# Second layer: key and query projections of one pair with high and low parts of x in one 512-column matmul

## The chip, the cores and the metric

The kernel runs on one core of one Trainium2 chip. The metric is the device time of one execution in microseconds (us). Three executions of the kernel before took 2110.76, 2111.51 and 2111.34 us, median 2111.34.

## The reference

Two conditioned transformer blocks in fp32, one after the other, on x of 64 sequences, 128 rows, 512 features, with a condition vector of 1024 per sequence. The first block has linear attention with 8 heads, the second has softmax attention with 16 heads of 32 features. The second block is the one that matters here:

```python
xn = layer_norm(x, norm_w, norm_b)
q = (xn @ q_w + q_b).reshape(Bx, Tx, H, -1)
k = (xn @ k_w + k_b).reshape(Bx, Tx, H, -1)
att = softmax(einsum('bnhl,bmhl->bnmh', q, k) + (1 - mask) * -1e6, axis=2)
y = einsum('bnmh,bmhl->bnhl', att, v).reshape(Bx, Tx, Dx)
h = layer_norm(y, sb_norm_w, sb_norm_b) * (1 + scale) + shift
return x + silu(h) @ out_w + out_b
```

`v` is a third projection of `xn`; `scale` and `shift` come from the condition vector.

## The kernel before, in words

Sequences go in pairs: 32 pairs through the first layer, then 32 pairs through the second. A tile has 128 partitions; D = 512 features are C = 4 chunks of 128, `b` is the sequence in the pair. The x of the next pair is loaded, normalised and transposed while the present pair is in attention.

Every projection is made from two parts of each operand. `xT_hi` is x in the reduced type fp32r, `xT_lo` is the rest, and the same for the weights `w_hi` and `w_lo`. The product is hi·hi + lo·hi + hi·lo, so three matmuls for each chunk, accumulated in one PSUM bank. `project_features` (L539) does this for keys and queries, with the weights stationary and 256 columns of x (2 sequences of 128) moving: one block `f` of 128 output features fills half a bank of 512 columns. `project_rows` (L531) does it for values and the output, with x stationary and 512 columns of weights moving.

Each engine has a program of its own, in one fixed order, and semaphores order them against one another. There is no planner. In the second layer each pair `i` has two steps, one for each of its sequences:

- `step0` (TensorE, L1752): scores of sequence 0, output of the previous pair's sequence 0, values, transposes of z, of prob and of the next x (`x_transposed`), output of the previous pair's sequence 1, mixing (`mixed`).
- `step1` (TensorE, L1780): scores of sequence 1; then keys of the next pair, blocks 0 and 1 woven with the four transposes of y (`turned`), blocks 2 and 3; transposes of z (`z_transposed`, L1631); query blocks 0 and 1; the 16 transposes of prob (`prob_turned`); query blocks 2 and 3; `mixed`.

The banks: 0 to 3 hold scores, then transposed prob. 4 is for y, 7 for z, 5 and 6 for keys, then queries, values, x (5, 7) and output (6).

VectorE in `step1` (L1432): maxima of score banks 0, 1, 2 (L1342); `end_outputs` (L1346: reciprocal of the sums, z from y, its statistics); maximum of bank 3; `keys_out` for blocks 0 and 1 (L1327: bank plus bias into `qk`); `end_norm` (L1370: normalise z, after GpSimd's 1/sqrt, L1234); `keys_out` 2 and 3; statistics of the x after next (`row_stats`); `end_silu`; `norm`; `low_part`.

ScalarE in `step1` (L1597): copy of y; 16 exponentials with their sums (`exps`, four heads for each bank); `gate` for z (L1530, four operations that read the transposed z); tanh; `queries_out` 0, 1 (L1498); copy of prob bank 0; `h_high`; the other three copies of prob; `queries_out` 2, 3.

`step1` of the first pair (`first`) also has the second layer's gains in it: TensorE transposes them (`emb.turned`) into bank 7, VectorE takes them out in eight small operations (`leave_bank`, L508), and makes them up (`gains`, L518). The last pair has no next one, so its `step1` projects nothing. So 31 of 32 pairs have the projections in `step1`.

Of the kernel before, what the change touches and what calls it, by code (L numbers as in the profile page):

```python
# [44 lines left out]
def build(nc, T, out):  # L45
# [15 lines left out]
    with root:  # L61
# [30 lines left out]
        m.xT_hi = sb("xT_hi", [P, C, PAIR, P], F32R)  # L92
        m.xT_lo = sb("xT_lo", [P, C, PAIR, P], F32R)
# [43 lines left out]
        def vcol(name, c):  # L137
# [11 lines left out]
            "x_biased", "qk_ps", "k", "q", "masks_in", "v_ps", "v", "s_ps", "top", "prob", "pT_ps", "pT",  # L149
# [990 lines left out]
def layer1(nc, m, s0, s, ps, T, emb, x1_d, out, x_in, mask_d, vec_rows, vcol, B, NP, D, C, HC, H, DH):  # L1140
# [33 lines left out]
    Y_BANK, Z_BANK, O_BANK = 4, 7, 6  # L1174
    QK_BANKS, V_BANKS, X_BANKS = (5, 6), (5, 6), (5, 7)
# [3 lines left out]
    def qk_banks(pair, n):  # L1179
        return FIRST_QK_BANKS[n] if isinstance(pair, int) and pair == 0 else QK_BANKS  # L1180
# [124 lines left out]
    def vector(dve):  # L1305
# [21 lines left out]
        def keys_out(pair, chunks):  # L1327
            banks = qk_banks(pair, K)
            for c in chunks:
                if c % 2 == 0:  # L1330
                    dve.wait_ge(s["qk_ps"], seq(C, pair, c // 2 + 1))
                at = (c % 2) * PAIR * P
                done = nc.vector.tensor_scalar(qk[:, K, c].rearrange("p b t -> p (b t)"),
                                               ps[banks[c // 2]][:, at:at + PAIR * P], qk_bias[:, K, c:c + 1],
                                               None, ALU.add)
                if c % 2:
                    done.then_inc(s["k"], 1)
# [94 lines left out]
        def step1(i, first, more, last):  # L1432
            maxima(i, 1, (0, 1, 2))
            end_outputs(i, 0)
            maxima(i, 1, (3,))
            if first:
                emb.leave_bank(dve, ps[Z_BANK])
            if not last:
                keys_out(i + 1, (0, 1))
            end_norm(i, 0)  # L1440
            if first:
                emb.gains(dve)
            if not last:
                keys_out(i + 1, (2, 3))
# [24 lines left out]
        keys_out(0, range(C))  # L1469
# [22 lines left out]
    def scalar(act):  # L1492
# [5 lines left out]
        def queries_out(pair, chunks):  # L1498
            banks = qk_banks(pair, Q)
            for c in chunks:  # L1500
                if c % 2 == 0:
                    act.wait_ge(s["qk_ps"], seq(C, pair, 2 + c // 2 + 1))
                at = (c % 2) * PAIR * P
                done = nc.scalar.activation(qk[:, Q, c].rearrange("p b t -> p (b t)"),
                                            ps[banks[c // 2]][:, at:at + PAIR * P], ACT.Identity,
                                            bias=qk_bias[:, Q, c:c + 1])
                if c % 2:
                    done.then_inc(s["q"], 1)

        def exps(i, b, first):  # L1510
            for a in range(HC):
# [18 lines left out]
        def gate(prev, b, bank=Z_BANK):  # L1530
# [47 lines left out]
        queries_out(0, (0, 1))  # L1578
        yield
        queries_out(0, (2, 3))  # L1580
# [16 lines left out]
        def step1(i, first, last):  # L1597
            copy_yT(i, 0)
            exps(i, 1, first)
            gate(i, 0)  # L1600
            tanh(i, 0)
            if not last:
                queries_out(i + 1, (0, 1))
            prob_out(i, 1, (0,))
            h_high(i, 0)
            prob_out(i, 1, (1, 2, 3))
            if not last:
                queries_out(i + 1, (2, 3))
# [15 lines left out]
    def tensor(pe):  # L1624
# [6 lines left out]
        def z_transposed(prev, b, bank=Z_BANK):  # L1631
# [13 lines left out]
        def projected(pair, n, chunks):  # L1645
            banks = qk_banks(pair, n)
            for f in chunks:
                dst = ps[banks[f // 2]][:, (f % 2) * PAIR * P:(f % 2 + 1) * PAIR * P]
                done = None
                for done in project_features(nc, w_hi, w_lo, n, f, xT_hi, xT_lo, dst, C, True):  # L1650
                    yield
                if f % 2:
                    done.then_inc(s["qk_ps"], 1)
# [7 lines left out]
        def scores(i, b):  # L1661

            if b == 0:
                pe.wait_ge(s["masks_in"], seq(16 * HC, i, 16 * HC))
                pe.wait_ge(s["q"], seq(2, i, 2))
                pe.wait_ge(s["k"], seq(2, i, 2))
# [21 lines left out]
        def mixed(i, b, first):  # L1688

            pe.wait_ge(s["v"], seq(PAIR, i, b + 1))  # L1690
            if b == 1:
                pe.wait_ge(s["y"], seq(PAIR, i, 1))
            elif not first:
# [47 lines left out]
        run(projected(0, K, range(C)))  # L1741
        pe.wait_ge(s["lo_qk"], 2)
        run(projected(0, Q, (0, 1)))
        yield
        run(projected(0, Q, (2, 3)))
# [34 lines left out]
        def step1(i, first, last):  # L1780
# [5 lines left out]
            else:  # L1786
                pe.wait_ge(s["xT_lo"], seq(PAIR, i + 1, PAIR))
                if first:
                    emb.turned(pe, ps[Z_BANK])
                woven(projected(i + 1, K, (0, 1)), turned(i, 0))  # L1790
                if not first:
                    pe.wait_ge(s["out"], seq(PAIR, i - 1, PAIR))
                run(projected(i + 1, K, (2, 3)))
                if first:
                    pe.wait_ge(emb.s["scale"], 1)
                z_transposed(i, 0)
                pe.wait_ge(s["k"], seq(2, i + 1, 1))
                run(projected(i + 1, Q, (0, 1)))
                prob_turned(i, 1, range(HC))
                pe.wait_ge(s["k"], seq(2, i + 1, 2))  # L1800
                run(projected(i + 1, Q, (2, 3)))
# [41 lines left out]
```

## Time and profile before

| | before |
|---|---|
| median of 3 executions | 2111.34 us |
| profiled execution, its own time | 2112.14 us |
| its span | 2110.3 us |
| mean granted TensorE clock | 0.996 |
| TensorE busy | 2071.9 us (98%) |
| VectorE busy | 1395.6 us (66%) |
| ScalarE busy | 1155.9 us (55%) |
| GpSimd busy | 581.8 us (28%) |

The span runs from the first to the last instruction; the execution's own time has 1.8 us around it. The second layer begins at about 1012 us. The busy time of TensorE includes the modelled ends of its matmuls, which overlap, so the distance between two starts is the price of a matmul, not its own duration. Granted clock is a share of 2.4 GHz.

### The profile page before, as it was taken

The page shows a single profiled execution, that of the slowest core. Times are in us where ns is not written, and L with a number is a line of the kernel's source. Part 1 is how long each engine was busy: PE and PEld are TensorE (multiplying, and loading weights), DVE is VectorE, ACT ScalarE, POOL GpSimd, SP SyncE. Part 2 cuts the span into 40 slices and gives each one's busy share as a digit, 9 for nine tenths or more (in the row PEclk, how much of TensorE's full clock was granted, in tenths as well). Part 3 has the DMA queues.
Part 4 walks back from the last instruction along what each step waited for, and adds up shares of the span by engine and source line. Part 5 has one row for each costly group of instructions (what it writes and reads, how often), then busy time and mean ns, then how long its engine had stood idle before and what let it go on. Part 6 is the DMA issues. An engine that isn't in the chain of part 4 may idle for free. (4 is left out here: it accounts for less than half of the span.)

```text
span 2110.3 us, 48285 instructions
## 1 busy us (share of the span) xinstructions
PE 2071.9 (98%) x17499; PEld 1824.0 (86%) x17499; DVE 1395.6 (66%) x2985; ACT 1155.9 (55%) x3816; POOL 581.8 (28%) x861
## 2 busy tenths in 40 slices
PE   7999999999999999999999999999999999999996
PEld 4888888888888888888798989899898989899895
DVE  6777777777777777776565656666565556656553
ACT  3333433343333433344677777777777777777774
POOL 4233323333233322334222222222222222222220
PEclk9999999999999999999999999999999999999998
DMA  6310001101110011102210101101010100101000
GB/s 214 110 40 30 35 35 40 40 25 35 40 40 31 33 35 40 40 25 76 66 36 25 35 25 35 40 22 38 25 35 25 35 29 31 40 25 35 25 26 21
DMA packets 52164, 86.43 MB, mean 41 GB/s; under 512 B 5667, under 2 KB 14565, under 8 KB 52134
## 3 DMA queue, kind: packets, MB, share of 16 engines
q1 hardware_dynamic: 52118, 86.03, 11.9%
q8 instruction: 19, 0.31, 0.1%
q14 instruction: 11, 0.09, 0.0%
q10 hardware_dynamic: 16, 0.00, 0.0%
HBM read 52.32 MB, written 33.69 MB: 41 GB/s over the span
## 5 line engine op out<-in xcount | busy, mean ns | idle before, releaser
L543 PE MATMUL bank<-xT_hi,w_hi 128*128 128x256 f32 x1536 | 449.4, 293 | 0.0
L544 PE MATMUL bank<-xT_lo,w_hi 128*128 128x256 f32 x1536 | 439.8, 286 | 0.0
L545 PE MATMUL bank<-xT_hi,w_lo 128*128 128x256 f32 x1536 | 437.0, 284 | 0.0
L1515 ACT ACTIVATE heads<-bank,top 128x128 f32<-128x128 f32 x1024 | 358.2, 402 | 100.5 <-DVE top L1342 100.5
L534 PE MATMUL bank<-w_hi,xT_hi 128*128 128x512 f32 x768 | 306.3, 399 | 4.4 <-DVE bias_all L395 4.4
L536 PE MATMUL bank<-w_lo,xT_hi 128*128 128x512 f32 x768 | 301.9, 393 | 0.0
L535 PE MATMUL bank<-w_hi,xT_lo 128*128 128x512 f32 x768 | 301.1, 392 | 0.0
L543 PEld LDWEIGHTS bank<-xT_hi,w_hi 128*128 128x128 f32 x1536 | 293.1, 191 | 6.2 <-issue 1.6
L544 PEld LDWEIGHTS bank<-xT_lo,w_hi 128*128 128x128 f32 x1536 | 293.4, 191 | 0.8 <-issue 0.8
L545 PEld LDWEIGHTS bank<-xT_hi,w_lo 128*128 128x128 f32 x1536 | 293.6, 191 | 0.0
L1342 DVE TENSOR_REDUCE top<-bank 128x4 f32<-128x512 f32 x256 | 162.7, 677 | 179.7 <-PE bank L1675 179.7
L927 ACT ACTIVATE heads<-bank,k_neg 128x128 f32<-128x128 f32 x256 | 70.1, 370 | 355.6 <-DVE k_neg L792 355.6
L1515 ACT ACTIVATION_READ_ACCUMULATOR heads<-bank,top 128x1 f32 x1024 | 248.5, 243 | 0.0
L534 PE MATMUL bank<-w_hi,h_hi 128*128 128x512 f32 x512 | 217.6, 425 | 9.1 <-DVE h_lo L1381 5.1
L535 PE MATMUL bank<-w_hi,h_lo 128*128 128x512 f32 x512 | 212.0, 414 | 0.0
L536 PE MATMUL bank<-w_lo,h_hi 128*128 128x512 f32 x512 | 206.2, 403 | 0.0
L534 PEld LDWEIGHTS bank<-w_hi,xT_hi 128*128 128x128 f32 x768 | 144.8, 189 | 33.0 <-DVE bias_all L395 4.9
L536 PEld LDWEIGHTS bank<-w_lo,xT_hi 128*128 128x128 f32 x768 | 144.6, 188 | 31.2
L535 PEld LDWEIGHTS bank<-w_hi,xT_lo 128*128 128x128 f32 x768 | 144.9, 189 | 28.6 <-issue 0.2
L695 POOL TENSOR_TENSOR h_lo<-ends,h_hi 128x512 fp32r<-128x512 f32 x64 | 86.8, 1376 | 219.9 <-ACT h_hi L953 219.9
L1522 ACT ACTIVATE heads<-bank 128x512 f32<-128x512 f32 x256 | 141.3, 599 | 2.8 <-PE bank L1685 2.3
L1232 POOL TENSOR_TENSOR ve_y<-mv_y,eps 128x1 f32<-128x1 f32 x64 | 12.2, 190 | 424.0 <-DVE mv_y L1360 424.0
(201 smaller groups left out, 4057.5 us busy)
## 6 DMA issues: line engine op xcount, KB each, us to landing
xr<-in_x SPq DMA_DIRECT2D x32, 512.0 KB, 3.4
x_between_layers<-ends SPq DMA_DIRECT2D x64, 256.0 KB, 2.0
xr<-x_between_layers SPq DMA_DIRECT2D x32, 512.0 KB, 4.1
out<-ends SPq DMA_DIRECT2D x64, 256.0 KB, 2.1
store<-in_L_cond_W_emb SPq DMA_DIRECT2D x4, 1024.0 KB, 12.1
store<-in_L_cond_emb_w SPq DMA_DIRECT2D x3, 1024.0 KB, 8.3
mask_rows<-mask_parts SPq DMA_DIRECT2D x128, 2.0 KB
heads<-in_L_cond_Wk SPq DMA_DIRECT2D x1, 1024.0 KB, 6.9
```

The source lines that it names most:

```text
L534: yield nc.tensor.matmul(bank[:, :], a_hi[:, c, b, :], w_hi[:, m, c, :], start=(c == 0), stop=False)
L535: yield nc.tensor.matmul(bank[:, :], a_lo[:, c, b, :], w_hi[:, m, c, :], start=False, stop=False)
L536: yield nc.tensor.matmul(bank[:, :], a_hi[:, c, b, :], w_lo[:, m, c, :], start=False, stop=(c == C - 1))
L543: yield nc.tensor.matmul(dst, w_hi[:, m, c, fs], a_hi[:, c], start=(first and c == 0), stop=False)
L544: yield nc.tensor.matmul(dst, w_hi[:, m, c, fs], a_lo[:, c], start=False, stop=False)
L545: yield nc.tensor.matmul(dst, w_lo[:, m, c, fs], a_hi[:, c], start=False, stop=(last and c == C - 1))
L695: nc.gpsimd.tensor_tensor(h_lo[:, :, b, :], hs[:, b], f32(h_hi[:, :, b, :]), ALU.subtract).then_inc(s["h_lo"], 1)
L927: last = nc.scalar.activation(k_exp[:, c, b, :], ps[j][:, at:at + P], ACT.Exp, bias=k_neg[:, c, b:b + 1])
L1232: nc.gpsimd.tensor_tensor(ve_y[:, b:b + 1], mv_y[:, b, 1:2], eps[:, 0:1], ALU.add).then_inc(s["y_var_eps"], 1)
L1342: nc.vector.tensor_reduce(top[:, b, C * a:C * a + C], ps[a][:, :].rearrange("p (c t) -> p c t", c=C), AX_X, ALU.max, negate=True).then_inc ...
L1515: last = nc.scalar.activation(prob[:, a, c, :], ps[a][:, c * P:(c + 1) * P], ACT.Exp, bias=top[:, b, h:h + 1], accum_out=total[:, b, h:h + 1])
L1522: nc.scalar.activation(prob_T[:, a], ps[a][:, :].rearrange("p (c t) -> p c t", c=C), ACT.Copy).then_inc(s["pT"], 1)
```

## The change

- `xT_hi` and `xT_lo` become views of one tile `xT`, laid out chunk, part (high, low), sequence, row.
- For all pairs but the first, key blocks 0 to 3 and query blocks 0 and 1 go through `project_wide`: for each chunk one matmul of `w_hi` with the 512 columns of high and low x, into a whole bank, and one of `w_lo` with the 256 columns of high x, into the bank's lower half. The block is then the sum of the bank's halves.
- ScalarE writes lower half plus bias into `qk` (`lower_out`), then VectorE adds the upper half to it (`block_out`). Query blocks 2 and 3 stay in the old form (`narrow`), in the halves of bank 5, and ScalarE copies both (`queries_out`).
- Banks: keys 5, 6, 7, 5; queries 6, 7, 5, 5. z of sequence 0 is transposed into bank 4, of sequence 1 into bank 7.
- TensorE's `step1`: key 0 woven with y's transposes, keys 1, 2, 3, z, queries 0, 1, prob, queries 2, 3. New waits: for VectorE's first key block before key 3, second before query 0, third before query 1; for the gates before `mixed` of sequence 1; in the first pair the gains leave bank 7 before key 2 rather than before z.
- VectorE's and ScalarE's `step1` get a new order, shown below. Semaphores `k`, `q` and `qk_ps` count blocks, not pairs of blocks; `lower` is new.

```diff
+def project_wide(nc, w_hi, w_lo, m, f, both, dst, C):
+    fs = slice(f * P, (f + 1) * P)
+    n = PAIR * P
+    for c in range(C):
+        yield nc.tensor.matmul(dst[:, :], w_hi[:, m, c, fs], both[:, c].rearrange("p h b t -> p (h b t)"),
+                               start=(c == 0), stop=False)
+        yield nc.tensor.matmul(dst[:, 0:n], w_lo[:, m, c, fs], both[:, c, 0].rearrange("p b t -> p (b t)"),
+                               start=False, stop=(c == C - 1))
...
+    Z_BANKS = (4, 7)
+    QK_BANKS, V_BANKS, X_BANKS = ((6, 7, 5, 5), (5, 6, 7, 5)), (5, 6), (5, 7)
...
+        def block_out(pair, n, f):                                   # VectorE
+            dst = qk[:, n, f].rearrange("p b t -> p (b t)")
+            dve.wait_ge(s["lower"], seq(C + 2, pair - 1, (K, Q).index(n) * C + f + 1))
+            nc.vector.tensor_tensor(dst, ps[QK_BANKS[n][f]][:, PAIR * P:2 * PAIR * P], dst,
+                                    ALU.add).then_inc(s["k" if n == K else "q"], 1)
...
         def step1(i, first, more, last):                            # VectorE
             maxima(i, 1, (0, 1, 2))
+            if not last:
+                block_out(i + 1, K, 0)
             end_outputs(i, 0)
             maxima(i, 1, (3,))
             if first:
+                emb.leave_bank(dve, ps[EMB_BANK])
+            if not last:
+                block_out(i + 1, K, 1)
             end_norm(i, 0)
+            if not last:
+                block_out(i + 1, K, 2)
+                block_out(i + 1, K, 3)
             if first:
                 emb.gains(dve)
             if more:
                 row_stats(i + 2, slot_of(i + 2))
+            if not last:
+                block_out(i + 1, Q, 0)
             end_silu(i, 0)
+            if not last:
+                block_out(i + 1, Q, 1)
             if more:
                 norm(i + 2, slot_of(i + 2))
             low_part(i, 0)
...
+        def lower_out(pair, n, f):                                   # ScalarE
+            act.wait_ge(s["qk_ps"], seq(EACH, pair, (K, Q).index(n) * C + f + 1))
+            nc.scalar.activation(qk[:, n, f].rearrange("p b t -> p (b t)"), ps[QK_BANKS[n][f]][:, 0:PAIR * P],
+                                 ACT.Identity, bias=qk_bias[:, n, f:f + 1]).then_inc(s["lower"], 1)
...
         def step1(i, first, last):                                  # ScalarE
             copy_yT(i, 0)
+            exps(i, 1, first, (0, 1))
+            if not last:
+                lower_out(i + 1, K, 0)
+            exps(i, 1, first, (2,))
+            if not last:
+                lower_out(i + 1, K, 1)
+                lower_out(i + 1, K, 2)
+            exps(i, 1, first, (3,))
+            if not last:
+                lower_out(i + 1, K, 3)
             gate(i, 0)
             tanh(i, 0)
+                lower_out(i + 1, Q, 0)
             prob_out(i, 1, (0,))
             h_high(i, 0)
+            prob_out(i, 1, (1,))
+                lower_out(i + 1, Q, 1)
+            prob_out(i, 1, (2, 3))
+                queries_out(i + 1, 2)
+                queries_out(i + 1, 3)
...
+                woven(projected(K, 0), turned(i, 0))                 # TensorE, step1
                 if not first:
                     pe.wait_ge(s["out"], seq(PAIR, i - 1, PAIR))
+                else:
+                    emb.turned(pe, ps[EMB_BANK])
+                run(projected(K, 1))
                 if first:
                     pe.wait_ge(emb.s["scale"], 1)
+                run(projected(K, 2))
+                pe.wait_ge(s["k"], seq(C, i + 1, 1))
+                run(projected(K, 3))
                 z_transposed(i, 0)
+                pe.wait_ge(s["k"], seq(C, i + 1, 2))
+                run(projected(Q, 0))
+                pe.wait_ge(s["k"], seq(C, i + 1, 3))
+                run(projected(Q, 1))
                 prob_turned(i, 1, range(HC))
+                pe.wait_ge(s["k"], seq(C, i + 1, C))
+                narrow(Q, 2)
+                narrow(Q, 3)
```

## Rows read from the trace of the kernel before

**Rows 1.** Busy time by stretch: us, then per engine busy (instructions), granted clock, DMA.
```profile
1400.00:2100.00 700.00, 689.76 (x6832) 618.16 (x6824) 411.93 (x831) 505.49 (x1887) 154.00 (x257) 0.99 0.09 30
...
1004.00:1012.00 8.00, 7.99 (x34) 6.49 (x35) 1.44 (x2) 0.00 (x0) 2.34 (x3) 1.00 0.78 262
2083.70:2095.30 11.60, 9.44 (x63) 7.76 (x64) 2.45 (x5) 6.45 (x19) 0.00 (x0) 0.65 0.01 1
```

**Rows 2.** Waits of TensorE, whole span: us in total, times, longest.
```profile
PE bank L1635 <- DVE z L1372: 5.9, 3, 4.8
```

**Rows 3.** Timeline of TensorE, one pair: start, duration, line, tiles, count [idle before].
```profile
1501.63 0.50 PE L1669 MATMUL bank<-mask_rows,one_rows 2*128 2x512 f32 x4
...
1504.10 0.28 PE L545 MATMUL bank<-xT_hi,w_lo 128*128 128x256 f32 x1
...
1509.14 0.28 PE L545 MATMUL bank<-xT_hi,w_lo 128*128 128x256 f32 x1
1509.26 0.60 PE L1635 MATMUL bank<-ident,z 128*128 128x128 f32 x4
...
1517.27 1.08 PE L1698 MATMUL bank<-heads,v 128*32 128x128 f32 x32
1518.28 0.50 PE L1669 MATMUL bank<-mask_rows,one_rows 2*128 2x512 f32 x4
```

**Rows 4.** Timeline of TensorE, value rows of the next step.
```profile
1522.95 0.40 PE L534 MATMUL bank<-w_hi,xT_hi 128*128 128x512 f32 x1
...
1525.49 0.39 PE L536 MATMUL bank<-w_lo,xT_hi 128*128 128x512 f32 x1
```

**Rows 5.** Timeline of VectorE in the same pair.
```profile
1500.90 0.69 DVE L1389 TENSOR_TENSOR ends<-bank,xr 128x512 f32<-128x512 f32 x1 [1.41 <-issue]
1503.06 1.89 DVE L1342 TENSOR_REDUCE top<-bank 128x4 f32<-128x512 f32 x3 [1.47 <-PE bank L1675]
1504.86 0.24 DVE L1348 RECIPROCAL p_sum<-total 128x16 f32<-128x16 f32 x1
...
1506.75 0.66 DVE L1342 TENSOR_REDUCE top<-bank 128x4 f32<-128x512 f32 x1
1507.33 0.87 DVE L1333 TENSOR_SCALAR pairs<-bank,qk_bias 128x256 f32<-128x256 f32 x2
1508.11 0.54 DVE L1372 TENSOR_SCALAR z<-z,mv_y,rstd_y 128x512 f32<-128x512 f32 x1
```

**Rows 6.** Timeline of ScalarE in the same pair.
```profile
1503.78 0.37 ACT L1515 ACTIVATE heads<-bank,top 128x128 f32<-128x128 f32 x1 [1.42 <-DVE top L1342]
...
1506.54 0.41 ACT L1515 ACTIVATE heads<-bank,top 128x128 f32<-128x128 f32 x1
...
1509.96 1.50 ACT L1536 ACTIVATE gates<-bank,gains 128x128 f32<-128x128 f32 x4 [0.49 <-PE bank L1635]
1511.49 0.63 ACT L1542 ACTIVATE gates<-gates 128x512 f32<-128x512 f32 x1
...
1514.50 1.58 ACT L1522 ACTIVATE heads<-bank 128x512 f32<-128x512 f32 x3
1517.38 0.84 ACT L1504 ACTIVATE pairs<-bank,qk_bias 128x256 f32<-128x256 f32 x2 [1.30 <-PE bank L545]
```

**Rows 7.** Timeline of GpSimd in the same pair.
```profile
1507.18 0.55 POOL L1234 TENSOR_TENSOR rstd_y<-ve_y,neg_half 128x1 f32<-128x1 f32 x1
```

**Rows 8.** Timeline of VectorE in the first pair.
```profile
1032.93 0.27 DVE L514 TENSOR_SCALAR store<-bank,vec 128x64 f32<-128x64 f32 x1
...
1034.36 0.25 DVE L522 TENSOR_SCALAR half_gain<-store,vec 128x64 f32<-128x64 f32 x1
```

**Rows 9.** Timeline of TensorE at three places where it idled.
```profile
1004.01 0.49 PE L534 MATMUL bank<-w_hi,h_hi 128*128 128x512 f32 x1 [2.39 <-POOL h_lo L695]
...
1044.57 0.50 PE L1669 MATMUL bank<-mask_rows,one_rows 2*128 2x512 f32 x4 [0.86 <-DVE w_lo L1395]
...
2083.74 1.12 PE L1635 MATMUL bank<-ident,z 128*128 128x128 f32 x4 [4.75 <-DVE z L1372]
```

More of the change, by code:

```diff
@@ L1325, in x_low, with first_keys_out @@
                                     f32(xT_hi[:, :, b, :]), ALU.subtract).then_inc(s["xT_lo"], 1)
[L1327 to L1337, printed above, removed]
+        def first_keys_out():
+            for c in range(C):
+                dve.wait_ge(s["qk_ps"], c // 2 * 2 + 2)
+                nc.vector.tensor_scalar(qk[:, K, c].rearrange("p b t -> p (b t)"), first_block(K, c),
+                                        qk_bias[:, K, c:c + 1], None, ALU.add).then_inc(s["k"], 1)
+        def block_out(pair, n, f):
[3 more added lines that the diff above has]
+                                    ALU.add).then_inc(s["k" if n == K else "q"], 1)
         def maxima(i, b, some):
@@ L1468, in vector @@
         yield
-        keys_out(0, range(C))
+        first_keys_out()
         low(V)
@@ L1496, in x_high, with first_queries_out, queries_out, exps @@
                                  ACT.Copy).then_inc(s["xT_hi"], 1)
-        def queries_out(pair, chunks):
-            banks = qk_banks(pair, Q)
+        def first_queries_out(chunks):
             for c in chunks:
[L1501 to L1511, printed above, removed]
+                act.wait_ge(s["qk_ps"], C + c // 2 * 2 + 2)
+                nc.scalar.activation(qk[:, Q, c].rearrange("p b t -> p (b t)"), first_block(Q, c), ACT.Identity,
+                                     bias=qk_bias[:, Q, c:c + 1]).then_inc(s["q"], 1)
+        def lower_out(pair, n, f):
+            act.wait_ge(s["qk_ps"], seq(EACH, pair, (K, Q).index(n) * C + f + 1))
+            nc.scalar.activation(qk[:, n, f].rearrange("p b t -> p (b t)"), ps[QK_BANKS[n][f]][:, 0:PAIR * P],
+                                 ACT.Identity, bias=qk_bias[:, n, f:f + 1]).then_inc(s["lower"], 1)
+        def queries_out(pair, f):
+            act.wait_ge(s["qk_ps"], seq(EACH, pair, EACH))
+            at = (f % 2) * PAIR * P
+            nc.scalar.activation(qk[:, Q, f].rearrange("p b t -> p (b t)"),
+                                 ps[QK_BANKS[Q][f]][:, at:at + PAIR * P], ACT.Identity,
+                                 bias=qk_bias[:, Q, f:f + 1]).then_inc(s["q"], 1)
+        def exps(i, b, first, some=range(HC)):
+            for a in some:
                 act.wait_ge(s["top"], seq(PAIR * C, i, b * C + a + 1))
@@ L1528, in copy_yT, with gate @@
                                  ACT.Copy).then_inc(s["yT"], 1)
-        def gate(prev, b, bank=Z_BANK):
+        def gate(prev, b, bank=None):
+            bank = Z_BANKS[b] if bank is None else bank
             if b == 0:
@@ L1629, in x_transposed, with z_transposed @@
             last.then_inc(s["xT_ps"], 1)
-        def z_transposed(prev, b, bank=Z_BANK):
+        def z_transposed(prev, b, bank=None):
+            bank = Z_BANKS[b] if bank is None else bank
             pe.wait_ge(s["z"], seq(PAIR, prev, b + 1))
@@ L1643, in out_rows, with first_projected, projected, narrow @@
             done.then_inc(s["o_ps"], 1)
-        def projected(pair, n, chunks):
-            banks = qk_banks(pair, n)
+        def first_projected(n, chunks):
             for f in chunks:
[L1648 to L1653, printed above, removed]
+                run(project_features(nc, w_hi, w_lo, n, f, xT_hi, xT_lo, first_block(n, f), C, True))\
+                    .then_inc(s["qk_ps"], 1)
+        def projected(n, f):
+            done = None
+            for done in project_wide(nc, w_hi, w_lo, n, f, m.xT, ps[QK_BANKS[n][f]], C):
+                yield
+            done.then_inc(s["qk_ps"], 1)
+        def narrow(n, f):
+            dst = ps[QK_BANKS[n][f]][:, (f % 2) * PAIR * P:(f % 2 + 1) * PAIR * P]
+            run(project_features(nc, w_hi, w_lo, n, f, xT_hi, xT_lo, dst, C, True)).then_inc(s["qk_ps"], 1)
         def value_rows(i, b):
@@ L1740, in tensor @@
         pe.wait_ge(s["lo_qk"], 1)
-        run(projected(0, K, range(C)))
+        first_projected(K, range(C))
         pe.wait_ge(s["lo_qk"], 2)
-        run(projected(0, Q, (0, 1)))
+        first_projected(Q, (0, 1))
         yield
-        run(projected(0, Q, (2, 3)))
+        first_projected(Q, (2, 3))
         pe.wait_ge(s["lo_vo"], 1)
```

42 lines of the change are left out of this document (15 added, 27 removed).

## The prediction

> **What bounds the kernel now.** I read the busy shares by stretch first. In 700 us of the second layer TensorE is busy 98.5% at full clock, ScalarE 72%, VectorE 59% [rows 1]. The list of waits says the same from the other side: over the whole span the transposes of z wait for VectorE only 3 times out of 64 [rows 2], and the one place of a pair where TensorE's stream waits at all is before the scores: ScalarE's last query copies end at 1517.38 + 0.84 = 1518.22 and the scores start at 1518.28, 0.2 us later than the matmuls before them would let them [rows 3, 6]. So TensorE's issue order is the clock of the layer, and an edit is worth what it does to TensorE's stream. Then I read the timeline of one pair, the steady step 1 that begins with the scores at 1501.63 and ends with the next scores at 1518.28 (16.65 us) [rows 3]. All 31 steps 1 that project a next pair have this shape; the last pair has none.
>
> The point to see there is how closely the other engines feed that stream. The z transposes start at 1509.26, and VectorE's z was written from 1508.11 for 0.54 us, to 1508.65 [rows 3, 5]. Today that is 0.5 us early. There is no other slack on this chain, and the edit adds to exactly this chain.
>
> **The edit on TensorE.** Of 32 blocks-by-chunks of keys and queries per pair (8 blocks, 4 chunks) 24 now issue one 512-column and one 256-column matmul in place of three 256-column ones. The columns streamed are the same, 768. From 1504.10 to 1509.14 are 42 intervals of 256 columns, so 120.0 ns each; from 1522.95 to 1525.49 are 11 intervals of 512 columns, so 230.9 ns each [rows 3, 4]. One merge saves 240.0 - 230.9 = 9.1 ns, so 16 merges in the keys save 0.15 us and 8 in the queries 0.07 us. That is 0.22 us a pair, 6.8 us over 31 pairs, and it is all that the edit can give. From below I take nothing saved (a 512 followed by a 256 with another weight has no row). The four transposes of y woven into the first key block cost what they cost today. The new order of banks adds TensorE no wait of its own in the keys: bank 6 is free at 1501.59 (VectorE's addition to the output starts at 1500.90 and takes 0.69) and is wanted only after the first key block [rows 5].
>
> In sentences of their own: the Trainium skill ("TensorE: Matmul & The Clock Gate", Back-to-back issue gap) gives N/2.4 ns + 2.5 ns between warm matmuls, thus 109.2 and 215.8 ns, and a merge would save only 2.6 ns. The rows do not agree with its size, they show 9.1 ns. By that rule the queries' part would be 0.02 us in place of 0.07 and the sum below 1.6 us longer.
>
> **The edit on VectorE and ScalarE, up to z.** This is the term that decides. VectorE's program after the maxima of score banks 0 to 2 was: reciprocal, z product, its statistics, maximum of bank 3, two key blocks, normalise z. Now the addition for key block 0 stands ahead of the reciprocal. It waits for ScalarE's lower half of that block, and ScalarE issues it only after the exponentials of banks 0 and 1. Both queues run in order, so everything of z stands behind it. Step by step, in the times of the pair shown:
> - The three maxima start at 1503.06 and take 1.89, to 1504.95 [rows 5].
> - The first exponential starts at 1503.78, the ninth at 1506.54 [rows 6]. ScalarE's lower half takes the ninth's place at 1506.54. Two copies of that size take 0.84 [rows 6], one alone about 0.47, so it ends at 1507.01. TensorE had finished that block long before, near 1505.
> - VectorE, idle since 1504.95, starts the addition at 1507.06. No row has a 256-wide addition from a bank and SBUF. Bounds: two 256-wide ones with a scalar take 0.87, 0.4 each in a row, and a 512-wide addition 0.69 [rows 5]. I take 0.43, nearer the row of the same width. Then the reciprocal starts at 1507.48 against 1504.86 before [rows 5]: 2.62 late. The same number with the bounds: 2.58 to 2.9.
> - The maximum of bank 3 moves from 1506.75 to 1509.37, and what follows it from 1507.33 to 1509.95 [rows 5]. That is now one key addition, 0.43, to 1510.38, where two copies took 0.78 to 1508.11. GpSimd's 1/sqrt lies beside it: 1507.18 + 0.55 + 2.62 = 1510.35 [rows 7]. So normalising z starts at 1510.40 and ends at 1510.94.
> - TensorE comes to the z transposes at 1509.26 - 0.15 = 1509.11 if the keys run through. They now start at 1511.00 for the weights, 1511.09 for the first transpose: 1.83 later than today, a stall of nearly 2 us. The keys' 0.15 us is thereby worth nothing.
>
> The fourth key block has a new wait too, for VectorE's first addition: it is out at about 1507.55, TensorE arrives at about 1507.6. This is a tie. If it is late by 0.2 us nothing changes, as z is later still.
>
> **After z.** The queries' 0.07 us is kept: net +1.76 us a pair. Does anything come later than this? Each other chain, in absolute times:
> - Exponentials of bank 3: their maximum ends at 1510.03, so they run 1510.08 to 1511.46, then a lower half to 1511.9, then the four gates (1.50 us [rows 6]) and tanh 0.63 [rows 6]. The gates were released at 1509.96 by the z transposes, now at 1511.8. So they are late by 1.9 and no more.
> - Behind tanh (1513.9 + 0.1) ScalarE has a lower half of queries 0.45, prob copy 0.55, h_hi about the same, prob copy 0.55, lower half 0.45, two prob copies 1.1 (three take 1.58 [rows 6]). VectorE's silu comes between, behind its own addition for query block 0, which costs ScalarE some 0.3. That ends near 1518.2. TensorE wants these copies for the mixing at 1517.27 + 1.76 = 1519.03 [rows 3]. Cover of 0.8 us. Its new wait for the gates, in front of the same matmuls, is met at 1513.3.
> - The last two query blocks end as before, ScalarE copies them as before (0.84 us from 1517.38 [rows 6]) beside the 1.01 us of mixing, and the scores wait the same 0.2 us.
>
> So ScalarE's four added copies (6 + 2 against 4, about 1.7 us) and VectorE's two added operations cost nothing by their busy time, because ScalarE idles 1.3 us before the last copies and VectorE 1.47 before the maxima [rows 5, 6]. What is paid is where they wait. Rearranging high and low of x into one tile changes the stride of the writes from 256 to 512 elements with the same runs of 128, in both layers. I take 0. First-pair copies signal per block rather than per two, also 0.
>
> **The first pair** has more behind the same wait. VectorE's eight unloadings of the gain bank end at 1032.93 + 0.27 = 1033.20 [rows 8], now 2.6 later at 1035.8; TensorE's third key block waits for them, where before only the z transposes did. Third and fourth block take 2.8: 1038.7. ScalarE must have the third block, exponentials of bank 3 (1.38) and the fourth block before VectorE's addition, which ends near 1040.2. Only then come the gains. From the start of the gains to the scores of the next pair are 1044.57 - 1034.36 = 10.21 us, all one chain (the last wait there is for VectorE's low part of the output weight) [rows 8, 9]. That gives 1050.4. Two more additions that wait for ScalarE, less the two copies of 0.8 now done, put about 1.9 on top: 1052.3, so +7.7. Bounds 5.9 and 11, the upper with a lowered clock, since TensorE has done its second block near 1031.5 and idles 4.3 us.
>
> **The sum.** The profiled execution took 2112.14 us, its span 2110.3; 1.8 lie around it and stay. 30 x 1.76 + 7.7 = 60.5. So 2172.6 for such an execution; it stands 0.8 above the median of 2111.34, so I predict 2111.34 + 60.5 = 2172. Bounds of the forecast: additions at 0.40 or 0.69 (two in z's chain, so -0.06 or +0.5 a pair), no saving in the queries +0.07, hand-overs of 0.03 or 0.08 us at four places, -0.1 or +0.1, the lower half 0.42 or 0.55. Together 1.5 to 2.4 a pair, 2111 + 45 + 5.9 = 2162 to 2111 + 72 + 11 = 2194. They won't all go one way: 2163 to 2187 for the likeliest case alone.
>
> **Rivals.**
> - The hold-up is small, and the saved issue time decides: faster. The place is VectorE's wait for the first lower half. If it took no more than 0.7 us (0.5 slack of z and 0.2 saved), the stall goes and every pair wins 0.22: 2111.3 - 6.8 = 2104.5, or about 2110 with some loss left in the first pair. For it: VectorE idles 1.47 us before the maxima and has room. Against it: the wait is 2.1 us long by two rows of ScalarE, eight exponentials of 0.345, and nothing could shorten these. 4%.
> - Part of the stall is won back, since ScalarE and VectorE enter step 0 with the same idle time as before and some wait today hides in TensorE's stream (0.2 us before the scores). Then +0.2 to +1.3 a pair, 2120 to 2155. Against it: only 0.2 us is there to give. 6%.
> - The chain behind tanh outgrows its cover of 0.8 us, because query additions and silu wait for one another on two engines. For it: five hand-overs between them. At 1.3 us longer than I have it, the mixing is 0.5 later: +15, 2187. 10%.
> - The granted clock falls after each stall. TensorE idled 2.39 us before 1004.01 and the clock stayed at its upper level, 2.4 GHz; it idled 4.75 before 2083.74, and then the mean over 11.6 us was 0.65, thus part of it at 1.2 GHz; four transposes took 1.12 us against 0.60 [rows 1, 3, 9]. My stall, 1.9 us, is nearer the first. If it fell, some 3 us of work at half speed lose about 1.6: +50, 2222. 4%.
>
> **Chances.** The forecast 76%, the rivals as given. 0.2% is 4 us, about what a measurement of this kernel can tell from no change. Faster by more than that: 4%, cut to 3 for the first pair's loss. Within it: 2%. Slower: 95%. The range 2155 to 2190 leaves out the faster case, most of the partial one, the clock, and some of the tail above the third.
>
> **What would show it.** In the changed kernel's timeline: VectorE idle about 2.1 us between the third maximum and the addition for key block 0, released by ScalarE; the reciprocal 2.6 us later after the scores than now; TensorE idle 1.8 to 2.0 us before the z transposes, released by VectorE's z, 30 times; steps 1 of 18.4 us from scores to scores, steps 0 unchanged; 512- and 256-column matmuls 0.351 us a couple; clock near 1. It is wrong if the z transposes don't wait, or if TensorE idles mainly somewhere else, as ahead of the mixing or of the fourth key block.

## The result, and the profile after

The changed kernel takes 2173.89 us (median of 4, 2169.82 to 2174.64) beside 2111.05 us (4 executions, 2110.51 to 2111.51). The ratio is 1.0295, with a 95% interval of 1.0279 to 1.031. The profiled execution took 2174.64 us with a span of 2172.8, so the spans differ by 62.5 us.

A first cut by the starts of the scores' mask matmuls shows where this lies. A pair is one step 1 and the step 0 behind it.

| stretch | before, us | after, us | difference |
|---|---|---|---|
| all up to the scores of the first pair's step 1 | 1025.89 | 1025.99 | 0.1 |
| first pair's step 1 | 18.68 | 27.69 | 9.0 |
| the step 0 behind it | 17.22 | 18.79 | 1.6 |
| 30 steady pairs | 1015.21 (33.84 each) | 1065.02 (35.50 each) | 49.8 |
| from the last step 1 to the end | 33.3 | 35.3 | 2.0 |

The same stretches in the busy times by stretch (us; then busy and instructions of TensorE, its weight loads, VectorE, ScalarE, GpSimd; granted clock; DMA), against the first of [rows 1]:

```profile
1025.99:1053.68 27.69, 19.06 (x173) 16.58 (x169) 17.69 (x49) 16.27 (x53) 4.77 (x7) 0.94 0.01 1
1053.68:1072.47 18.79, 18.79 (x148) 15.50 (x148) 10.07 (x18) 11.51 (x44) 5.14 (x9) 0.91 0.04 15
1072.47:2137.49 1065.02, 1013.44 (x9356) 868.98 (x9352) 621.90 (x1281) 785.52 (x2878) 216.81 (x383) 1.00 0.09 29
1400.00:2100.00 700.00, 666.53 (x6133) 572.18 (x6134) 412.03 (x850) 518.38 (x1892) 147.99 (x260) 1.00 0.09 29
```

TensorE's busy time in the 700 us fell from 689.76 to 666.53, so it now idles 33 us there. Fewer pairs fit into 700 us than before, so the added work of the others has to be read over the 30 steady pairs. The row of the kernel before for them is

```profile
1061.79:2077.00 1015.21, 1014.48 (x10076) 911.74 (x10072) 605.99 (x1221) 738.82 (x2758) 231.85 (x383) 1.00 0.09 31
```

Thus ScalarE has 46.7 us more work in them and VectorE 15.9. The first number is close to the 49.8 us that the pairs lost, so a comparison of busy times alone can't tell a wait from work; the experiments do. The mean clock in the steady pairs rounds to 1.00. The list of waits names the two ends of the chain (total us, times, longest):

```profile
DVE pairs L1354 <- ACT pairs L1530: 156.5, 125, 2.1
...
PE bank L1680 <- DVE z L1390: 56.6, 32, 4.8
```

The z transposes waited 5.9 us in 3 places before [rows 2]; now 56.6 us in 32, which are the 30 steady pairs and two places behind the last step 1. One pair of the trace, TensorE's timeline, to be laid beside [rows 3]; step 1 starts at 1498.42 here and at 1501.63 there:

```profile
1498.42 0.51 PE L1719 MATMUL bank<-mask_rows,one_rows 2*128 2x512 f32 x4
...
1504.36 0.28 PE L556 MATMUL bank<-xT,w_lo 128*128 128x256 f32 x1
1504.48 0.39 PE L554 MATMUL bank<-xT,w_hi 128*128 128x512 f32 x1
...
1505.75 0.28 PE L556 MATMUL bank<-xT,w_lo 128*128 128x256 f32 x1
1507.73 0.66 PE L1680 MATMUL bank<-ident,z 128*128 128x128 f32 x4 [1.70 <-DVE z L1390]
1508.14 0.48 PE L554 MATMUL bank<-xT,w_hi 128*128 128x512 f32 x1
...
1511.05 1.91 PE L1735 MATMUL bank<-ident,heads 128*128 128x128 f32 x16
...
1515.76 1.08 PE L1749 MATMUL bank<-heads,v 128*32 128x128 f32 x32
1516.77 0.50 PE L1719 MATMUL bank<-mask_rows,one_rows 2*128 2x512 f32 x4
```

Step 1 takes 1516.77 - 1498.42 = 18.35 us, where it took 16.65. TensorE idles 1.70 us ahead of the z transposes and nowhere else in the step: key block 3 (1504.48) follows key block 2 without a gap. VectorE and ScalarE in the same pair, beside [rows 5] and [rows 6]:

```profile
1499.84 1.89 DVE L1360 TENSOR_REDUCE top<-bank 128x4 f32<-128x512 f32 x3 [1.46 <-PE bank L1725]
1503.88 0.42 DVE L1354 TENSOR_TENSOR pairs<-bank,pairs 128x256 f32<-128x256 f32 x1 [2.15 <-ACT pairs L1530]
1504.22 0.24 DVE L1366 RECIPROCAL p_sum<-total 128x16 f32<-128x16 f32 x1
...
1506.11 0.66 DVE L1360 TENSOR_REDUCE top<-bank 128x4 f32<-128x512 f32 x1
1506.69 0.41 DVE L1354 TENSOR_TENSOR pairs<-bank,pairs 128x256 f32<-128x256 f32 x1
1507.13 0.55 DVE L1390 TENSOR_SCALAR z<-z,mv_y,rstd_y 128x512 f32<-128x512 f32 x1
```

```profile
1500.57 0.37 ACT L1545 ACTIVATE heads<-bank,top 128x128 f32<-128x128 f32 x1 [1.42 <-DVE top L1360]
...
1503.33 0.52 ACT L1530 ACTIVATE pairs<-bank,qk_bias 128x256 f32<-128x256 f32 x1
...
1513.57 1.08 ACT L1552 ACTIVATE heads<-bank 128x512 f32<-128x512 f32 x2
```

VectorE ends the three maxima at 1501.73 and idles 2.15 us. ScalarE's first lower half takes the ninth place behind eight exponentials at 1503.33, the addition starts at 1503.88, and the reciprocal is at 1504.22. From the start of step 1 that is 5.80, against 3.23 before: 2.57 us late.

### The profile page after: what moved, and what is told of

Read it like the earlier page. It is cut to its first block and busy times, and to the rows that moved or that the text cites. A ratio compares the mean times of both kernels' runs of the same rounds, so it can differ in the third digit from the quotient of the medians.

```text
span 2172.8 us, 47415 instructions
## 1 busy us (share of the span) xinstructions
PE 2075.7 (96%) x16755; PEld 1783.0 (82%) x16755; DVE 1413.0 (65%) x3047; ACT 1205.0 (55%) x3940; POOL 566.2 (26%) x861
## 5 line engine op out<-in xcount | busy, mean ns | idle before, releaser
L534 PE MATMUL bank<-w_hi,xT 128*128 128x512 f32 x768 | 306.1, 399 | 4.5 <-DVE bias_all L395 4.5
L536 PE MATMUL bank<-w_lo,xT 128*128 128x512 f32 x768 | 301.8, 393 | 0.0
L535 PE MATMUL bank<-w_hi,xT 128*128 128x512 f32 x768 | 300.7, 392 | 0.0
L554 PE MATMUL bank<-xT,w_hi 128*128 128x512 f32 x744 | 277.5, 411 | 4.1 <-DVE store L514 4.1
L1545 ACT ACTIVATION_READ_ACCUMULATOR heads<-bank,top 128x1 f32 x1024 | 241.3, 236 | 0.0
L543 PE MATMUL bank<-xT,w_hi 128*128 128x256 f32 x792 | 230.2, 291 | 0.0
L544 PE MATMUL bank<-xT,w_hi 128*128 128x256 f32 x792 | 223.7, 282 | 0.0
L545 PE MATMUL bank<-xT,w_lo 128*128 128x256 f32 x792 | 223.3, 282 | 0.0
L556 PE MATMUL bank<-xT,w_lo 128*128 128x256 f32 x744 | 213.4, 287 | 0.0
L1354 DVE TENSOR_TENSOR pairs<-bank,pairs 128x256 f32<-128x256 f32 x186 | 78.5, 422 | 156.5 <-ACT pairs L1530 156.5
L534 PEld LDWEIGHTS bank<-w_hi,xT 128*128 128x128 f32 x768 | 144.8, 189 | 33.0 <-DVE bias_all L395 4.9
L536 PEld LDWEIGHTS bank<-w_lo,xT 128*128 128x128 f32 x768 | 144.5, 188 | 31.4
L554 PEld LDWEIGHTS bank<-xT,w_hi 128*128 128x128 f32 x744 | 140.3, 189 | 35.4 <-DVE store L514 4.4
L535 PEld LDWEIGHTS bank<-w_hi,xT 128*128 128x128 f32 x768 | 144.7, 188 | 28.6 <-issue 0.2
L543 PEld LDWEIGHTS bank<-xT,w_hi 128*128 128x128 f32 x792 | 150.4, 190 | 2.5 <-issue 1.6
```

Of the source, the lines that this page charges most:

```text
L534: yield nc.tensor.matmul(bank[:, :], a_hi[:, c, b, :], w_hi[:, m, c, :], start=(c == 0), stop=False)
L535: yield nc.tensor.matmul(bank[:, :], a_lo[:, c, b, :], w_hi[:, m, c, :], start=False, stop=False)
L536: yield nc.tensor.matmul(bank[:, :], a_hi[:, c, b, :], w_lo[:, m, c, :], start=False, stop=(c == C - 1))
L554: yield nc.tensor.matmul(dst[:, :], w_hi[:, m, c, fs], both[:, c].rearrange("p h b t -> p (h b t)"), start=(c == 0), stop=False)
L556: yield nc.tensor.matmul(dst[:, 0:n], w_lo[:, m, c, fs], both[:, c, 0].rearrange("p b t -> p (b t)"), start=False, stop=(c == C - 1))
L1354: nc.vector.tensor_tensor(dst, ps[QK_BANKS[n][f]][:, PAIR * P:2 * PAIR * P], dst, ALU.add).then_inc(s["k" if n == K else "q"], 1)
```

## The experiments

The theory is that VectorE's addition for key block 0, standing ahead of z's chain and waiting for ScalarE, is the loss in the steady pairs. Its rivals are the extra work of ScalarE and VectorE, and the wide matmul itself. Each kernel was measured beside the kernel before on the same chip, and the ratios are to that. Its median was 2113.38 us beside the wait alone, the shortened wait, the split in the changed kernel and z's chain first; 2113.70 beside the shorter wait, the first pair alone and the two kernels with both orders; 2112.09 beside the last.

**The wait alone, in the kernel before**

```diff
             maxima(i, 1, (0, 1, 2))
+            if not last:
+                dve.wait_ge(s["prob"], seq(PAIR * C, i, C + 2))
             end_outputs(i, 0)
```

> The kernel before, with nothing but a wait added: in step 1 VectorE waits, ahead of the reciprocal of end_outputs, until ScalarE has done the exponentials of score banks 0 and 1 (31 pairs). No wide matmul, no addition, no lower half. Theory (VectorE's place in the order, held by ScalarE, is the whole loss): the reciprocal is 2.0 us later, z is released 1.5 us after TensorE wants it, steps 1 take 18.1 to 18.2 us in place of 16.65, and the time is 2111 + 30 x 1.5 + 3 or 4 in the first pair = 2159 (2153 to 2164). Rival (the wide matmuls or the added operations of ScalarE and VectorE cost the time): 2111 to 2115.

Measured 2158.78 us, ratio 1.0216 (1.0199 to 1.0234). VectorE's timeline, then TensorE's, in one pair:

```profile
1523.54 1.89 DVE L1342 TENSOR_REDUCE top<-bank 128x4 f32<-128x512 f32 x3 [1.47 <-PE bank L1677]
1527.19 0.25 DVE L1348 RECIPROCAL p_sum<-total 128x16 f32<-128x16 f32 x1 [1.77 <-ACT heads L1517]
...
1530.45 0.54 DVE L1372 TENSOR_SCALAR z<-z,mv_y,rstd_y 128x512 f32<-128x512 f32 x1
```

```profile
1522.11 0.50 PE L1671 MATMUL bank<-mask_rows,one_rows 2*128 2x512 f32 x4
...
1531.05 0.65 PE L1637 MATMUL bank<-ident,z 128*128 128x128 f32 x4 [1.15 <-DVE z L1372]
...
1540.12 0.50 PE L1671 MATMUL bank<-mask_rows,one_rows 2*128 2x512 f32 x4
```

VectorE idles 1.77 us where it idled none, TensorE 1.15 us before the z transposes, and a steady pair takes 35.21 us: +1.37, a little less than the 1.5 expected. Nothing of the change is in this kernel but the waiting, and it gives 45 us of the 62; in its trace 41.0 of the 49.8 us of the steady pairs, and 4.5 in the first pair.

**A shorter wait, in the kernel before**

```diff
             maxima(i, 1, (0, 1, 2))
+            if not last:
+                dve.wait_ge(s["prob"], seq(PAIR * C, i, C + 1))
             end_outputs(i, 0)
```

> The kernel before with nothing but a shorter wait added: VectorE waits ahead of end_outputs in step 1 for the exponentials of score bank 0 alone, some 0.5 us rather than 1.8. Theory (z has 0.5 us of slack today; the long wait cost 1.37 us a steady pair for a hold of 1.8 to 2.0): the hold is absorbed, steady pairs take 33.84 to 33.95 us, time 2111 to 2117 with what the first pair adds. Rival (any hold on VectorE at this place is paid in full): 30 x 0.5 = 15 us more, 2126.

Measured 2112.75 us, ratio 0.9999 (0.999 to 1.0008). VectorE's timeline:

```profile
1502.46 1.89 DVE L1342 TENSOR_REDUCE top<-bank 128x4 f32<-128x512 f32 x3 [1.47 <-PE bank L1677]
1504.73 0.26 DVE L1348 RECIPROCAL p_sum<-total 128x16 f32<-128x16 f32 x1 [0.38 <-ACT heads L1517]
...
1507.99 0.54 DVE L1372 TENSOR_SCALAR z<-z,mv_y,rstd_y 128x512 f32<-128x512 f32 x1
```

The hold is 0.38 us by the row, z is normalised 0.5 us later after the scores than before (6.96 against 6.48), and the steady pairs take 33.84 us as ever. The 0.5 us of slack that the prediction read in z's chain is there, and this hold, which uses it up, costs nothing in a steady pair. In the first pair's step 1 there is no such slack: TensorE waited 0.24 us for z already before, it waits 0.73 now, and the step takes 19.19 us in place of 18.68.

**The wait shortened in the changed kernel**

```diff
-            exps(i, 1, first, (0, 1))
+            exps(i, 1, first, (0,))
             if not last:
                 lower_out(i + 1, K, 0)
-            exps(i, 1, first, (2,))
+            exps(i, 1, first, (1, 2))
```

> The changed kernel with ScalarE's first lower half of the keys issued after the exponentials of bank 0 rather than of banks 0 and 1; VectorE's order is kept. A dose test: four exponentials fewer, 1.38 us, in front of the wait. Theory: VectorE's idle time before the first addition falls from 2.15 to about 0.8 us, the idle time before the z transposes from 1.70 to 0.35, and the time by 31 x 1.35 = 42 to 2132 (2126 to 2138). Rival (z's delay comes from the added operations rather than from the wait): within 6 us of 2174.

Measured 2138.47 us, ratio 1.0118 (1.0101 to 1.0135): 0.5 us above the range that was expected. VectorE idles 0.75 us before the addition, TensorE 0.54 before the z transposes, and a steady pair takes 34.33 us: 1.17 less than in the changed kernel for 1.40 us less waiting. The rest went into a second wait that the expectation had not seen: VectorE reaches the addition for key block 1 earlier and idles 0.27 us there for ScalarE's lower half of that block. The first pair keeps 7.7 us of its loss.

**512 columns split into twice 256, in the changed kernel**

```diff
-        yield nc.tensor.matmul(dst[:, :], w_hi[:, m, c, fs], both[:, c].rearrange("p h b t -> p (h b t)"),
-                               start=(c == 0), stop=False)
+        for h in range(2):
+            done = nc.tensor.matmul(dst[:, h * n:(h + 1) * n], w_hi[:, m, c, fs],
+                                    both[:, c, h].rearrange("p b t -> p (b t)"),
+                                    start=(c == 0 and h == 0), stop=False)
+        yield done
```

> The changed kernel with each 512-column matmul of the wide projection issued as two of 256 columns into the halves of the bank, everything else kept. Theory: in the keys the matmul time lies in front of a wait for z, so their part changes nothing; the queries' 8 merges cost 0.1 us back. Steps 1 take 18.4 to 18.5 us in place of 18.35, the idle time before the z transposes falls from 1.70 to about 1.4 to 1.5, time 2172 to 2178. Rival (the wide matmul is itself slow or holds something up): the time falls back by 10 us or more, below 2164.

Measured 2177.27 us, ratio 1.0301 (1.0284 to 1.0319). A steady pair takes 35.57 us, 0.07 more than with the 512-column form, and the idle time before z is 1.53 us rather than 1.70: the keys' matmul time is only waiting time in another shape. The wide matmul does not cost; it is hidden.

**z's chain first**

```diff
             maxima(i, 1, (0, 1, 2))
-            if not last:
-                block_out(i + 1, K, 0)
             end_outputs(i, 0)
             maxima(i, 1, (3,))
+            if not last:
+                block_out(i + 1, K, 0)
             if first:
                 emb.leave_bank(dve, ps[EMB_BANK])
-            if not last:
-                block_out(i + 1, K, 1)
             end_norm(i, 0)
             if not last:
+                block_out(i + 1, K, 1)
                 block_out(i + 1, K, 2)
```

> The changed kernel with VectorE's additions for the key blocks moved behind: maxima 0 to 2, end_outputs, maximum 3, key block 0, then z's normalising, then key blocks 1 to 3. Same operations, same counts on all engines. Theory: the 2.1 us of waiting and one addition leave z's chain, z is ready about 0.7 us before TensorE wants it, TensorE waits 0.1 to 0.3 us for key block 0 before key 3 instead, and the saved issue time shows: 2100 to 2110. Rival (more work on ScalarE and VectorE costs the time wherever it stands, the chain behind tanh outgrowing its cover): 2125 or more.

Measured 2121.32 us, ratio 1.0034 (1.0022 to 1.0047): a miss by 11 us, though over 50 us came back with every operation kept. The steady pairs take 33.84 us, exactly as in the kernel before, and ScalarE and VectorE have their added work in them, 780.77 and 622.86 us:

```profile
1072.39:2087.66 1015.27, 1014.52 (x9357) 870.97 (x9354) 622.86 (x1281) 780.77 (x2878) 217.49 (x383) 1.00 0.09 31
```

So the added work costs nothing where it stands, and the order was the loss. TensorE's timeline around the start of key block 3, where matmuls come in couples, one of 512 columns and one of 256:

```profile
1518.16 0.28 PE L556 MATMUL bank<-xT,w_lo 128*128 128x256 f32 x1
1518.39 0.50 PE L554 MATMUL bank<-xT,w_hi 128*128 128x512 f32 x1
...
1519.89 0.60 PE L1679 MATMUL bank<-ident,z 128*128 128x128 f32 x4
```

From 1518.16 to 1518.39 are 230 ns where a couple's second interval is 117, and its first matmul then takes 0.34 to the next start in place of 0.23: 0.22 us a pair, for key block 0, which VectorE has out only at 1518.33. That is all that the merges save. The 8 us by which the median stands above the kernel before lie in the first pair's step 1 (+6.7) and the step behind it (+1.6).

**The first pair alone**

```diff
+            if first:
+                maxima(i, 1, (0, 1, 2))
+                end_outputs(i, 0)
+                emb.leave_bank(dve, ps[EMB_BANK])
+                block_out(i + 1, K, 0)
+                maxima(i, 1, (3,))
+                end_norm(i, 0)
+                emb.gains(dve)
+                block_out(i + 1, K, 1)
+            else:
...
```

> The changed kernel with another VectorE order in the first pair's step 1 only: reciprocal and z's statistics, the gain bank's unloading, key block 0, maximum 3, z, the gains, key blocks 1 to 3. The 30 steady pairs keep the order of the change. Theory (of the 62.5 us between the two traced spans, 9.0 lie in the first pair's step 1 and 1.6 in the step after it, the rest in the steady pairs and 2 behind the last): that step 1 gets 7 to 9 us shorter, so 2162 to 2168, steady pairs at 35.50 us as before. Rival (the first pair's loss is the wide form's own, or is only moved into the second pair): over 2170.

Measured 2165.91 us, ratio 1.0244 (1.0229 to 1.026). The first step 1 takes 20.61 us in place of 27.69, the steady pairs 35.50 as before this edit. The step behind the first stays at 18.79. (The `else` branch, not shown, keeps the order of the change.)

**Both orders together, and what the merge gives there**

```diff
             maxima(i, 1, (0, 1, 2))
-            if not last:
-                block_out(i + 1, K, 0)
             end_outputs(i, 0)
-            maxima(i, 1, (3,))
             if first:
                 emb.leave_bank(dve, ps[EMB_BANK])
             if not last:
+                block_out(i + 1, K, 0)
+            maxima(i, 1, (3,))
+            end_norm(i, 0)
+            if first:
+                emb.gains(dve)
+            if not last:
                 block_out(i + 1, K, 1)
-            end_norm(i, 0)
-            if not last:
                 block_out(i + 1, K, 2)
                 block_out(i + 1, K, 3)
-            if first:
-                emb.gains(dve)
```

> The changed kernel with z's chain first in all pairs: maxima 0 to 2, end_outputs, key block 0, maximum 3, z, key blocks 1 to 3; the first pair as in the kernel with only that pair reordered. Unlike the kernel that had key block 0 behind maximum 3, key block 0 is out before TensorE ends key block 2, so neither wait is left. Theory: a steady pair takes 33.84 - 0.22 (the wait before key 3) - 0.03 = 33.6 us, and the first pair is within 1 us of the kernel before: 2103 to 2108 beside 2111. Rival (the wide form gives nothing even with all waits gone): 2111 or more.

Measured 2110.20 us, ratio 0.9985 (0.9976 to 0.9994). The steady pairs take 33.615 us, as expected, but the first pair and the step behind it still lose 1.9 + 1.6 us, so the median is 2 us above the range. VectorE's timeline in one pair:

```profile
1501.97 1.89 DVE L1360 TENSOR_REDUCE top<-bank 128x4 f32<-128x512 f32 x3 [1.47 <-PE bank L1724]
1503.78 0.24 DVE L1366 RECIPROCAL p_sum<-total 128x16 f32<-128x16 f32 x1
...
1506.01 0.42 DVE L1354 TENSOR_TENSOR pairs<-bank,pairs 128x256 f32<-128x256 f32 x1 [0.26 <-ACT pairs L1529]
...
1506.95 0.54 DVE L1390 TENSOR_SCALAR z<-z,mv_y,rstd_y 128x512 f32<-128x512 f32 x1
```

The wait before the addition is 0.26 us, and z is done 0.5 us before TensorE's transposes at 1508.00. The same kernel with the matmuls split as above:

> The kernel with z's chain first in all pairs and key block 0 ahead of maximum 3, and each 512-column matmul issued as two of 256 columns. It measures what the merge itself gives when nothing hides it. Theory (couples of 512 and 256 start 0.3465 us apart in the changed kernel's keys and 0.352 in its queries, three of 256 take 0.360): 16 x 0.0135 + 8 x 0.008 = 0.28 us a pair, 8 to 9 us more than the kernel with the 512-column matmuls. Rival (the prediction's 9.1 ns a merge): 6.8 us. Rival (nothing): the same time.

Measured 2116.65 us, ratio 1.0014 (1.0005 to 1.0023), steady pairs 33.83 us. The merge gives 0.215 us a steady pair, thus 6.5 us over 30 of them, and the medians of 11 executions each differ by 6.45. (The two profiled spans differ by 9.4: 4.6 us of it lie ahead of the first step 1, and in the step behind the first pair the split kernel was 1.6 us shorter by its clock, of which more below. Single spans are a coarse measure here.) That is the prediction's 0.22 and 6.8, at 9 ns a merge, and not the 0.28 and 8.7 that I expected here from the couples' starts in the changed kernel.

**The last wait of the first pair**

The edit is against the kernel with both orders.

```diff
             end_silu(i, 0)
+            if first:
+                low(O)
             if not last:
                 block_out(i + 1, Q, 1)
...
             low_part(i, 0)
-            if first:
-                low(O)
```

> The kernel with z's chain first in all pairs (512-column matmuls), and in the first pair VectorE makes the low part of the output weight (2.49 us) after the silu, where it otherwise idles 1.6 us for ScalarE, rather than last. Theory: TensorE's 1.65 us of idle time before the second pair's scores goes, and with it the lowered clock that the trace without this edit shows right behind it (0.66 over 5 us, the step 1.57 us longer than the kernel before's 17.22). First step 1: 19.0 us in place of 20.6; the step after it 17.2 to 17.3 in place of 18.8; together 3.2 us, a ratio to the kernel before of 0.997 (2105 to 2107.5 beside 2111 to 2113). Rival (the clock falls for another reason than that idle time): the step after stays at 18.8 and only 1.6 us are won.

Measured 2104.47 us, ratio 0.9968 (0.9956 to 0.998). The first step 1 takes 18.90 us and the step behind it 17.24, which is 0.2 us from the kernel before for the two; the steady pairs take 33.61, 6.95 us less over 30. The median is 0.5 us below the range, the ratio as expected. This is the fastest of all, 0.3% under the kernel before: the wide form pays once nothing waits in front of z.

## Why the prediction was right

**The chain to z.** The steps, as the prediction set them and as the trace has them, each from the start of step 1 (1501.63 in the prediction, 1498.42 after):

| step | predicted | measured |
|---|---|---|
| VectorE starts the first addition | 5.43 | 5.46 |
| reciprocal | 5.85 | 5.80 |
| z's normalising | 8.77 | 8.71 |
| first z transpose | 9.46 | 9.31 |
| step 1 in all | 18.41 | 18.35 |

The addition takes 0.42 us and holds the queue 0.34, where I had 0.43, and TensorE starts 0.60 us after the start of z's normalising, where I had 0.69. From the first z transpose on the pair shown takes 9.04 us, 0.09 more than predicted, so part of this goes again. In the mean a steady pair costs 1.66 and not 1.76, so 49.8 us and not 52.8.

**The wait, not the work.** It was said that ScalarE's and VectorE's added operations cost nothing by their busy time. The wait alone gives 1.37 of the 1.66 us; the kernel with z first has all the operations and steady pairs of 33.84 us, none of it lost. The remaining 0.3 us fit what the wait alone leaves out: with ScalarE's lower half and the addition the reciprocal comes 5.80 us into the step in place of 5.08, and one key operation fewer between it and z gives half of that back, so that z's normalising starts at 8.71 in place of 8.34. No run took these apart.

**The chains without a price** held. ScalarE's last prob copy ends at 1514.65 and the mixing starts at 1515.76, a cover of 1.1 us (0.8 predicted). The tie at key block 3 went the good way, and it became a wait of 0.22 us a pair as soon as the addition was put behind maximum 3. One reading of the prediction was wrong: the 0.2 us that TensorE was to wait for ScalarE's query copies before the scores. From the mixing to the scores are 1.01 us there (1517.27 to 1518.28), and 1.01 as well at the start of the same step (1500.62 to 1501.63), where ScalarE has no query copies in front. The sum doesn't use it.

**TensorE's saving** was 9.1 ns a merge from two cadences, 0.22 us a pair; the pair of kernels that differ in nothing else gives 0.215, or 9.0 ns. The Trainium skill ("TensorE: Matmul & The Clock Gate", Back-to-back issue gap) would have 2.6 ns a merge by its formula for isolated matmuls; the runs don't agree with that size.

**The first pair** is the term that was too small, 7.7 us in the sum and 9.0 + 1.6 measured, inside the bound of 11. Its chain is as told. What I left to the bound is the granted clock. TensorE's timeline there:

```profile
1035.93 0.51 PE L554 MATMUL bank<-xT,w_hi 128*128 128x512 f32 x1 [4.09 <-DVE store L514]
...
1036.40 0.39 PE L554 MATMUL bank<-xT,w_hi 128*128 128x512 f32 x1
1036.63 0.28 PE L556 MATMUL bank<-xT,w_lo 128*128 128x256 f32 x1
...
1037.18 0.63 PE L554 MATMUL bank<-xT,w_hi 128*128 128x512 f32 x1
1037.61 0.41 PE L556 MATMUL bank<-xT,w_lo 128*128 128x256 f32 x1
...
1040.38 0.61 PE L1680 MATMUL bank<-ident,z 128*128 128x128 f32 x4
...
1049.93 1.08 PE L1749 MATMUL bank<-heads,v 128*32 128x128 f32 x32 [1.53 <-ACT heads L1552]
1053.68 0.51 PE L1719 MATMUL bank<-mask_rows,one_rows 2*128 2x512 f32 x4 [2.66 <-DVE w_lo L1413]
```

TensorE idles 4.09 us, starts at full speed (a 512-column interval of 0.23 at 1036.40), and about 1 us after it resumed the interval is 0.43 (1037.18). So the third and fourth key block take 4.45 us (1035.93 to 1040.38) where the sum had 2.8; VectorE starts the gains at 1041.45 where it had 1040.2, and the next scores start at 1053.68 where it had 1052.3. Then TensorE idles 1.53 and 2.66 us, the 5 us from 1053.68 have a mean clock of 0.66, and the step behind takes 1.6 us more. Another 2.0 us lie behind the last step 1, where no projection is left and both kernels run the same idle times of 4.8 and 4.4 us, at a mean clock of 0.71 against 0.78. No run ties these to the change: the nine other kernels took 34.2 to 34.4 us there, between the 33.3 and the 35.3, and the two of them that are the kernel before with a wait took 34.4. So two errors met, 3 us too much in the steady pairs and 5 too little around them, 2 of which may be chance. That 60.5 came so near to 62.5 is in part luck; the 1.66 for 1.76 is not. The range holds either way, though the bounds as listed add up to 2.5 us a pair above, and not to 2.4.

**Rivals.** A small hold-up: the 2.15 us are what two rows of ScalarE said. A stall won back: no, and the 0.2 us that it was to come from are not there. The chain behind tanh: its cover was 1.1 us. The clock falling after each stall: 1.70 us of idle time 30 times, and the clock stayed at its upper level. Where it did fall, behind the first pair's 2.66 us, it cost the 1.6 us that this rival was priced at.

## What to carry to other kernels

When a result is made in two parts by two engines, look where the second part's instruction stands in its engine's order, and what stands behind it. Here an addition that could not start before 5.5 us into the step stood in front of a chain with 0.5 us of slack; with the chain ahead of it, it starts at the same 5.5 us, since it fills what was idle time. Read the slack from the trace before the edit, and place the waiting instruction by when its input comes and when its consumer wants it: ahead of the chain it cost 50 us, one maximum too late it cost the whole gain of the edit in the steady pairs.

## What the runs showed of the hardware

The granted clock does not follow the length of the last idle time alone. In the kernel with both orders and in its twin with split matmuls TensorE idled alike in the first pair (0.33, 0.92 and 1.65 us; 0.32, 0.91 and 1.66). The 5 us behind the last of these, in the one, in the other, and in the kernel without the last idle time:

```profile
1044.91:1049.91 5.00, 5.00 (x47) 4.04 (x48) 2.41 (x5) 2.32 (x14) 1.90 (x2) 0.66 0.01 3
```

```profile
1049.60:1054.60 5.00, 5.00 (x54) 4.18 (x55) 3.43 (x6) 2.81 (x17) 1.91 (x2) 1.00 0.01 3
```

```profile
1042.38:1047.38 5.00, 5.00 (x58) 4.16 (x55) 3.44 (x6) 3.38 (x18) 2.15 (x2) 1.00 0.01 3
```

The first has 0.66, the others 1.00, and the step is 18.81 against 17.24 us. In the kernel with only the first pair reordered, also with wide matmuls, it is 0.66 again. Taking the idle time away kept the clock; why the split kernel kept it with the idle time is open, as each is one profile. The kernel before with the wait alone shows the same from another side. In its first pair TensorE idled 2.12 us ahead of z, resumed at full speed, and about 1 us later the intervals of 256 columns went from 0.12 to 0.21 us. It then idled 2.02 us before the next scores, longer than the 1.65 above, and the 5 us behind that were at the upper level:

```profile
1047.29:1052.29 5.00, 5.00 (x54) 4.18 (x55) 3.44 (x6) 2.81 (x17) 0.00 (x0) 1.00 0.01 3
```

And 1.70 us of idle time ahead of z in each steady pair of the changed kernel left the mean clock at 1.00.
